# A relative attention's first unshifted scores made beside the phase before it, and a routing phase with its residual tiles made early

## What is computed

```python
# layer 2 (its attention is done before; this is the end of it and the MoE)
x = x + attention(h, ...)                       # ctx @ wo + bo
h = layernorm(x, ln2_scale, ln2_shift)
scores = h @ gate_w                             # 8 experts, the best 2 are taken
out = sum over the 2 experts of weight * (silu(h @ w1) * (h @ w2)) @ w3
# layer 3, relative attention with 16 heads of width 8
AC = einsum('bhid,bhjd->bhij', q + u_bias, k)
BD = _rel_shift(einsum('bhid,hjd->bhij', q + v_bias, rp))
attn = softmax((AC + BD) * scale);  out = attn @ v
```

## Time and profile before

| | |
|---|---|
| median of 3 runs | 1942.32 us (1934.86 to 1944.3) |
| profiled execution | 1947.51 us, of which 1945.9 us are the traced span |
| PE, DVE, ACT, POOL busy | 71%, 59%, 51%, 24% of the span |
| moved by DMA | 451.86 MB |
| `phase_route` to the start of `phase_blocks` | 535.5 to about 678 us |
| `phase_combine` | 828.1 to 959.6 us |
| `phase_relative` | 959.6 to 1833.3 us |

### The profile page before, as it was taken

One profiled execution on the slowest core, in us unless ns is written; L12 is line 12 of the kernel. 1 busy time (PEld: TensorE's weight loads), 2 busy tenths in 40 slices (PEclk: granted clock), 3 DMA queues, 4 the chain that ended last, 5 costly groups with the idle time before them and its releaser, 6 DMA issues. The chain is left out here.

```text
span 1945.9 us, 48913 instructions
## 1 busy us (share of the span) xinstructions
PE 1381.7 (71%) x18791; PEld 902.3 (46%) x18791; DVE 1147.5 (59%) x3054; ACT 1000.3 (51%) x1996; POOL 465.0 (24%) x762
## 2 busy tenths in 40 slices
PE   6636277777654269825458989888898989989646
PEld 3213144444334258713235655555555656556423
DVE  6953377777354223336326767766676766767637
ACT  4524056666612023313446767766676766767234
POOL 5443345555347610078000000000000000000033
PEclk9867589999955579966769999999998998999869
DMA  7429512222031176638899999999999999999531
GB/s 310 170 94 284 117 47 69 65 64 70 12 104 41 46 178 198 181 105 266 256 375 331 373 366 378 383 375 366 366 378 333 378 379 377 386 382 371 165 105 44
DMA packets 174816, 451.86 MB, mean 232 GB/s; under 512 B 41632, under 2 KB 133952, under 8 KB 157504
## 3 DMA queue, kind: packets, MB, share of 16 engines
q1 hardware_dynamic: 129488, 237.18, 37.1%
q10 hardware_dynamic: 32592, 180.39, 23.7%
q0 software_dynamic: 12512, 31.21, 6.0%
HBM read 222.59 MB, written 225.84 MB: 230 GB/s over the span
## 5 line engine op out<-in xcount | busy, mean ns | idle before, releaser
L2651 DVE CUSTOM_DVE_ANT_0 r_shifted<-r_ps_ac,r_shifted 128x512 f32<-128x512 f32 x512 | 351.9, 687 | 278.3 <-PE r_ps_ac L2530 236.4
L2617 ACT ACTIVATE r_probs<-r_ps_keys 128x512 f32<-128x512 f32 x512 | 309.6, 605 | 228.2 <-PE r_ps_keys L2537 203.3
L2596 ACT ACTIVATE r_wide<-r_ps_wide 128x512 f32<-128x512 f32 (+1 forms) x576 | 329.5, 590 | 63.6 <-PE r_ps_wide L2521 63.2
L2537 PE MATMUL r_ps_keys<-r_ident,r_shifted 128*128 128x128 f32 x2048 | 325.8, 283 | 16.8 <-issue 10.8
L2537 PEld LDWEIGHTS r_ps_keys<-r_ident,r_shifted 128*128 128x128 f32 x2048 | 267.4, 147 | 64.8 <-issue 19.6
L2521 PE MATMUL r_ps_wide<-r_r,r_qv 128*32 128x96 bf16 (+12 forms) x6144 | 235.7, 254 | 55.2 <-issue 40.3
L2659 DVE TENSOR_SCALAR r_shifted<-r_shifted,r_mx 128x512 f32<-128x512 f32 x512 | 249.2, 487 | 18.3
L985 ACT ACTIVATE c_probs<-c_ps_keys 128x512 f32<-128x512 f32 (+1 forms) x384 | 174.3, 530 | 130.9 <-PE c_ps_keys L911 130.7
L2530 PE MATMUL r_ps_ac<-r_k,r_qu 128*128 128x512 bf16 x512 | 207.8, 406 | 22.7 <-DMA r_k<-stack 20.6
L1190 POOL MEMSET n_zeros<- 128x4 f32 x1 | 0.1, 102 | 898.4 <-POOLq L2371 898.4
L2521 PEld LDWEIGHTS r_ps_wide<-r_r,r_qv 128*32 128x32 bf16 x6144 | 104.2, 98 | 153.2 <-issue 152.6
(11 more groups left out here) (253 smaller groups left out, 1920.3 us busy)
## 6 DMA issues: line engine op xcount, KB each, us to landing
skew<-r_wide ACTq DMA_DIRECT2D x64, 2224.0 KB, 13.5
r_shifted<-skew SPq DMA_DIRECT2D x64, 2160.0 KB, 14.4
by_expert<-a_blank ACTq DMA_DIRECT2D x4, 4352.0 KB
e_w<-in_L_ffn_w_dram SPq DMA_DIRECT2D x117, 128.0 KB, 2.4
c_qk<-qk_stacks POOLq DMA_DIRECT2D x64, 192.0 KB, 3.8
stack<-d_part SPq DMA_DIRECT2D x96, 128.0 KB
qk_stacks<-b_part SPq DMA_DIRECT2D x48, 128.0 KB, 3.3
qk_stacks<-b_part POOLq DMA_DIRECT2D x48, 128.0 KB, 3.7
```

Of the source, the lines that this page charges most:

```text
L2537: last = pe.transpose(ps_keys[u % 2][:, j * P:(j + 1) * P], shifted[:, s, W * u + j * P:W * u + (j + 1) * P], ident[:, :])
L2596: act.activation(wide[:, s, c, lo:hi], ps_wide[bk % BANKS][:, 0:hi - lo], ACT.Copy).then_inc(wide_sb, 1)
L2617: act.activation(probs[:, h % 2, :, b * P:(b + 1) * P], ps_keys[u % 2][:, :].rearrange("p (j i) -> p j i", j=NT), ACT.Exp, scale=SCALE).th ...
L2651: dve.tensor_tensor_reduce(out=shifted[:, s, W * u:W * u + L], in0=ps_ac[u % 2][:, :], in1=shifted[:, s, W * u:W * u + L], scale=1.0, scal ...
```

## The change

In `phase_route`: `xb` gets a tile for each batch and is made 2 ahead, then 3 batches at a time behind the roots of batches 0 and 1. The norm keeps two sets of moments and roots (`TurnNorm`). Minus the mean times the root is one instruction of DVE (`scale_means`), which stands behind `best` and ahead of `mark`, in place of two of POOL. The waits for the small tables move from the start of each engine's queue to their first use.

In `phase_combine`: the operands of step 0 (and the queries of step 1) are loaded behind batch 2's first two stores; the 18 banks of step 0 are made by PE and copied by ACT, five each in batches 3, 4 and 5 and three in batch 6; SP sends the two halves, in batches 5 and 7, ahead of those batches' `stack` stores. `phase_relative` starts with the fetches of step 0 and makes only step 1's banks ahead of its steps.

```diff
+def position_products(pe, ps, qv, r, s, g, c, bk):
+    lo, hi = BANK * bk, min(BANK * bk + BANK, CW)
+    for v in range(HT):
+        u = HT * c + v
+        h, b = u // NT, u % NT
+        for a in range(P // Q):
+            q0 = b * P + a * Q
+            start = W * v + P - Q - Q * a
+            split = start + q0 + Q
+            for one, frm, to in ((0, start, split), (1, split, start + W)):
+                frm, to = max(frm, lo), min(to, hi)
+                if frm < to:
+                    at = frm - start + L - Q - q0
+                    last = pe.matmul(ps[Q * a:Q * a + Q, frm - lo:to - lo], qv[:, s, h, q0 + one:q0 + one + Q],
+                                     r[:, g // 2, h, at:at + to - frm],
+                                     start=True, stop=True, skip_group_check=True)
+    return last
...
-                if n >= SLOTS:
-                    pool.wait_ge(xa_ready, n - SLOTS + 1)
-                pool.tensor_tensor(xb[:, n % SLOTS, :, :], x[:, n, :, :],
+                pool.tensor_tensor(xb[:, n, :, :], x[:, n, :, :],
...
-            AHEAD = 3
-            pool.memset(zeros[:, :], 0.0).then_inc(zeros_set, 1)
-            pool.wait_ge(zeros_set, 1)
+            AHEAD = 2
...
             for n in range(NB):
-                pool.wait_ge(norm.var_ready, n + 1)
-                pool.tensor_tensor(minus[:, n, :], zeros[:, :], norm.mv[:, :, 0], ALU.subtract)\
-                    .then_inc(minus_mean, 1)
-                if n >= 1:
-                    pool.wait_ge(z_ready, n)
-                norm.root(pool, n + 1)
-                pool.wait_ge(minus_mean, n + 1)
-                pool.wait_ge(norm.rstd_ready, n + 1)
-                pool.tensor_tensor(minus[:, n, :], minus[:, n, :], norm.rstd[:, :], ALU.mult)\
-                    .then_inc(minus_ready, 1)
-                if n + AHEAD < NB:
-                    add_bias(n + AHEAD)
+                if n >= 2:
+                    pool.wait_ge(z_ready, n - 1)
+                norm.root(pool, n)
+                for later in range(AHEAD + 3 * n, min(AHEAD + 3 * n + 3, NB)):
+                    add_bias(later)
                 if n >= 2:
                     scatter(n - 2)
...
-            pe.wait_ge(route_loaded, 16 * 5)
-            pe.wait_ge(patterns_set, 6)
-            pe.wait_ge(lower_set, 1)
...
                     invert(n + 2)
+                if n == 2:
+                    pe.wait_ge(patterns_set, 6)
+                    pe.wait_ge(lower_set, 2)
                 if n >= 2:
                     rank(n - 2)
+                if n == 1:
+                    pe.wait_ge(route_loaded, 16 * 5)
                 if n >= 1:
                     score(n - 1)
                 turn(n)
...
-                                  xb[:, n % SLOTS, :, :], ALU.add).then_inc(xa_ready, 1)
+                                  xb[:, n, :, :], ALU.add).then_inc(xa_ready, 1)
                 dve.wait_ge(xa_ready, n + 1)
-                if n >= 1:
-                    dve.wait_ge(minus_ready, n)
-                norm.moments(dve, xa[:, n % SLOTS, :, :], n + 1)
+                norm.moments(dve, xa[:, n % SLOTS, :, :], n)
...
+            def scale_means(n):
+                dve.wait_ge(norm.rstd_ready, n + 1)
+                dve.scalar_tensor_tensor(out=minus[:, n, :], in0=norm.mv[:, n % 2, :, 0], scalar=-1.0,
+                                         in1=norm.rstd[:, n % 2, :], op0=ALU.mult, op1=ALU.mult)\
+                    .then_inc(minus_ready, 1)
...
-            dve.wait_ge(route_loaded, 16 * 5)
-            dve.tensor_scalar(lower[:, :], mask[:, :], 0.0, None, ALU.is_lt).then_inc(lower_set, 1)
             divide(0)
             for n in range(NB):
                 if n + 1 < NB:
                     divide(n + 1)
                 merge(n)
+                if n == 0:
+                    dve.wait_ge(route_loaded, 16 * 5)
+                    dve.tensor_scalar(lower[:, :], mask[:, :], 0.0, None, ALU.is_lt).then_inc(lower_set, 1)
...
                     best(n - 1)
+                scale_means(n)
+                if n >= 1:
                     mark(n - 1)
...
+        BANKS = 3
+        ROWS = 64
+        WIDE_FROM = 3
+        WIDE_EACH = 5
...
+        def wide_banks(n):
+            first = WIDE_EACH * (n - WIDE_FROM)
+            return range(max(first, 0), max(min(first + WIDE_EACH, 2 * NBK), 0))
...
                 sp.dma_start(v9_out[n], v9[:, s, :, :]).then_inc(v_stored[s], 16)
+                if n == WIDE_FROM - 1:
+                    sp.wait_ge(stored[0], STORES)
+                    sp.wait_ge(act_stored[0], ACT_STORES)
+                    for g in range(2):
+                        sp.dma_start(qv_tile[ROWS * g:ROWS * g + SK, g, :, 0:L],
+                                     stacks_out[1].rearrange("b r (g h) t -> b g r h t", h=G)[0, g])\
+                            .then_inc(queries_loaded, 16)
+                    for dst, table in ((qu_tile, stacks_out[0]), (k_tile, stacks_out[2])):
+                        sp.dma_start(dst[0:SK, 0, :, :], table.rearrange("b r (g h) t -> b g r h t", h=G)[0, 0])\
+                            .then_inc(operands_loaded, 16)
+                for c in range(2):
+                    if n >= 1 and NBK * (c + 1) - 1 in wide_banks(n - 1):
+                        sp.wait_ge(wide_sb, NBK * (c + 1))
+                        dst = skew_out[c]
+                        sp.dma_start(bass.AP(tensor=dst.tensor, offset=dst.offset, ap=[[CW, P], [1, CW]]),
+                                     wide[:, c, :]).then_inc(sent, 16)
                 for c in range(NSP):
                     sp.wait_ge(part3_ready, NC * n + c + 1)
                     term_stores(sp, n, c, stored[s])
...
+            def wide_bank(i):
+                if i == 0:
+                    pe.wait_ge(queries_loaded, 32)
+                if i >= BANKS:
+                    pe.wait_ge(wide_sb, i - (BANKS - 1))
+                position_products(pe, ps_wide[i % BANKS], qv_tile, rel_r, 0, 0, i // NBK, i % NBK)\
+                    .then_inc(wide_ps, 1)
...
+            for ps in ps_wide:
+                for j in range(NT):
+                    pe.transpose(ps[:, j * P:(j + 1) * P], ident[:, :], ident[:, :])
             turn(0)
...
+                for i in wide_banks(n):
+                    wide_bank(i)
...
+            def copy_wide(i):
+                c, bk = i // NBK, i % NBK
+                act.wait_ge(wide_ps, i + 1)
+                lo, hi = BANK * bk, min(BANK * bk + BANK, CW)
+                act.activation(wide[:, c, lo:hi], ps_wide[i % BANKS][:, 0:hi - lo], ACT.Copy).then_inc(wide_sb, 1)
...
+                for i in wide_banks(n):
+                    copy_wide(i)
...
-            load_queries(0, 0)
-            load_queries(0, 1)
-            load(0, 0)
+            sp.sem_inc(stored, 64)
+            for s in range(2):
+                sp.sem_inc(qv_loaded[s], 16)
+            sp.sem_inc(loaded[0], 32)
+            for c in range(2):
+                sp.sem_inc(sent[0][c], 16)
+            fetch(0, 0, 0)
             load_values(0, 0)
-            sp.sem_inc(stored, 64)
-            for c in range(2):
-                fetch(0, 0, c)
-            sp.wait_ge(wide_ps, 2 * NBK)
+            fetch(0, 0, 1)
             load_queries(0, 2)
             load(0, 1)
...
-                last.then_inc(wide_ps, 1)
+                position_products(pe, ps, qv, r, s, g, c, bk).then_inc(wide_ps, 1)
...
-            for n in range(2):
-                pe.wait_ge(qv_loaded[n], 16)
-                for c in range(2):
-                    for bk in range(NBK):
-                        wide_bank(n, n, n, c, bk)
             pe.wait_ge(loaded[0], 32)
             content_tile(0, 0, 0)
             content_tile(0, 0, 1)
+            pe.sem_inc(wide_ps, 2 * NBK)
+            pe.wait_ge(qv_loaded[1], 16)
+            for c in range(2):
+                for bk in range(NBK):
+                    wide_bank(1, 1, 1, c, bk)
...
             steps(step, pe)```

In what follows, `x3` behind a row is a count. POOL's queue in `phase_route` (`m_norm_rstd` is a root, `m_xb` the residual plus bias of one batch, `by_expert` the 8 indirect transfers of one). Before, the rows of batch 2:

```order
L1465 TENSOR_TENSOR m_minus<-m_zeros,m_norm_mv 128x4
L123 TENSOR_TENSOR m_norm_var_eps<-m_norm_mv,m_norm_consts 128x4
L126 TENSOR_TENSOR m_norm_rstd<-m_norm_var_eps,m_norm_consts 128x4
L1472 TENSOR_TENSOR m_minus<-m_minus,m_norm_rstd 128x4
L1434 TENSOR_TENSOR m_xb<-m_x,m_bo 128x512
L1442 DMA by_expert<-m_z,m_pos 34816x128 x8
```

More of the change, by code:

```diff
@@ L41 @@
 CW = HT * W + P - Q
+BANK = 512
+NBK = -(-CW // BANK)
 REGION = NB * L
@@ L1893, in _, with phase_combine @@
             take_sums(BLOCKS - 1)
-def phase_combine(nc, sems, tiles, y_in, w_in, biases, tables, ident_in, x_out, stacks_out, v9_out):
+def phase_combine(nc, sems, tiles, y_in, w_in, biases, tables, ident_in, x_out, stacks_out, v9_out,
+                  relative):
     base, pos, pr = tiles
+    qu_tile, k_tile, qv_tile, rel_r, skew_out = relative
```

(12 more changed lines are left out.)

41 lines of the change are left out of this document (15 added, 26 removed).

## The result

The changed kernel takes 1929.35 us (median of 12 runs, 1916.28 to 1932.33) against 1945.69 (12 runs, 1934.86 to 1958.22): ratio 0.9898, interval 0.9873 to 0.9923. The ratio is not the quotient of the two medians, which is 0.9916: by the medians the change is 16 us faster, by the ratio 20 us, 0.8 to 1.0%. The forecast was 1922 in a range of 1908 to 1935. Three later sets of runs, each on another chip of the three, had the changed kernel in two of them: 0.9900 (0.9866 to 0.9935) in the second set and 1.0011 (0.9981 to 1.0041) in the third, where the gain is gone. Both have to be explained. The chip of the first result is not on record.

A forecast was written before the change was run, and what follows sets the result against it. DMA engines bound phase_relative, PE close behind; POOL bounds phase_route. Routing 8.9 plus combine and relative 11 gives 20 us off the profiled 1947.5, so 1927.5, or 1922 us against the median 1942.3; range 1908 to 1935.

The forecast's parts named there:

- Routing, 8.9 us: phase_route: earlier start 3.4 us, roots' batches 7.5 us, less 2.0 us of cost; between 2 and 12 us gained.
- the gaps between scatters: phase_route, POOL: without the additions and two minus instructions, the gaps between scatters shrink by 5.8 us in all.
- The chain for one batch: phase_route: best experts to next moments takes about POOL's new period, 11.6 us; the gain could fall to 4 us.
- The meeting: phase_route, batches 0 and 1: DVE's scale_means is released exactly when POOL begins xb, 1.0 us lost each.
- (c): phase_route: POOL's additions hold up scale_means in batches 0 and 1; first scatter 2 us later, 0 to 7 us.
- The banks, 0 (0 to 4): phase_combine: step 0's banks are hidden in PE's and ACT's slack and cost nothing, bounds 0 to 4 us.
- The cover is thin: phase_combine: slack barely hides ACT's added copies; at 0.7 us or more a bank, four batches slip about 1 us each.
- The sends, 7.5 us: End of phase_combine: 11 us for two sends less 3.6 us of idle DMA time; 7.5 us longer, 3 to 29.
- The start of relative, 11 us net: Start of phase_relative: idle DMA time and moved operand loads, 14.9 us less 4; 11 us gained, 4.1 to 23.8.
- PE's first bank of step 2: Start of phase_relative, a sign: this bank comes about 15 us behind the phase's start.
- PE's lead is kept: phase_relative, rival: held by PE's order as much as by DMA, PE's 23.8 us lead stays; 1908 us, chance 0.15.
- Slower through SP's blocked queue: phase_combine, rival: stores wait behind sends, combine ends 29 us later and more; 1952 us at 41 us delay, chance 0.05.

The follow-up runs named there:

- e3: The changed kernel with all eight residual tiles added on POOL ahead of the first root; 1931.82 us, ratio 0.9900 to before.
- e1: Before with the edits of phase_route alone; 1940.25 us, ratio 0.9952 to before.
- e10: Before with step 0's eighteen banks and operand loads also in combine, nothing sent, relative unedited, run in the third set; 1973.68 us, ratio 1.0143 to before.
- e6: Before with step 0's eighteen banks and operand loads also in combine, nothing sent, relative unedited, run in the first set; 1980.62 us, ratio 1.0150 to before.
- e7: Before with step 0's banks, loads and both sends from SP also in combine, relative unedited; 1978.84 us, ratio 1.0165 to before.
- e5: The changed kernel with step 2's queries and step 1's content operands issued ahead of the fetches in relative; 1921.57 us, ratio 0.9877 to before.
- e4: The changed kernel with both sends issued by ACT behind a half's last copy, in place of SP; 1922.40 us, ratio 0.9873 to before.
- e8: The changed kernel itself, run again in the third set; 1954.57 us, ratio 1.0011 to before.
- e9: Before with the edits of phase_combine and phase_relative alone, run in the third set; 1957.36 us, ratio 1.0024 to before.

## Why the prediction was right, and where it was not

**Routing, 8.9 us: right, 9.8.** Up to the first scatter 4.2 us (40.5 to 36.3 us into the phase) against 3.4 + 1.75 - 2.0 = 3.15; the rest in the gaps between scatters (5.6 against 5.8), which shrank to 1.53 us as the earlier trace rows said. The chain for one batch did not bite. The meeting came in both batches, in batch 1 on a cast of DVE ahead of `scale_means` (1.21 us, 0.18 in e3) and on the marks behind it (`x_hot` twice in 1.31 us, 0.29 in e3). The price (c) was still near 1 us net: the first projection came 3.6 us earlier in the phase, and 3.6 + 1.75 - 4.2 = 1.1. As I read it, e3's 2.2 us is the price against no meeting at all, and before had paid one already, the 1.19 us of `m_both`. The Trainium skill (SBUF — State Buffer, section "SBUF: two separate sides") has it, for a DVE instruction with two SBUF inputs, as a lock for a whole instruction: 1.23 us under POOL's addition and 0.16 without it agree. The cast has one input, so this part of the rule does not speak of it, and no run shows what held it. e1 gave 8.0 to 9.4 us by itself on a chip with late signals, whose trace has only 6.7 of it in routing.

**The banks, 0 (0 to 4): right in the result and the second set, wrong in the other two.** The step "The cover is thin: if a bank took 0.7 us or more, each of four batches would slip by about 1 us" named the right place and the wrong cause. A bank takes 0.5 us everywhere. What can be late is PE's signal, mostly by 2 to 7 us and at most by 11.5 (e10), and a batch with banks waits for several in a row where the old one had slack; the term is 21 us there (20.9 and 21.0 in e6 and e10). No row of before could show this, since its trace has no late signal.

**The sends, 7.5 us: right in the traces.** In the span of combine e7 less e6 gives 7.6 us, and 7.5 against e10; the whole times are too uncertain to show it. The whole growth of combine, 10.1 us, was under-sized by 2.6, which I put down to the border and the loads; no run separates these.

**The start of relative, 11 us net: right in size, or 3 us too high.** By the bytes of the first trace it is 21.3 - 10.1 = 11.2 us; by the three traces at before's rate it is 18 - 10.1 = 8 us. The forecast's own parts were 18.5 us off relative (11 + 7.5) and 7.5 on combine, so by these traces relative came out as summed and the 2.6 us too few of combine are the miss. The part was never timed by itself where no signal was late, so it rests on the phases and the bytes. PE's first bank of step 2 was forecast 15 us behind the phase's start and came at 25.7, since I had overlooked that in the new order its queries stand behind both fetches again. It cost nothing in the sum, because I had taken the sum from the DMA engines' time and not from PE's order, and e5 fits that: with the wait of 11.93 us gone 4 to 7 us come by the bytes.

**The rivals.** *PE's lead is kept* (1908) seemed true by the first trace, 24.6 us for combine and relative; 13 of it is the rate, and the medians, 16 and 20 us in all, leave 7 to 11 beside routing. *Slower through SP's blocked queue* falls with e4. What happened in the first and the third set, a new combine that eats the gain, was in none of them; its balance in e8: 4.3 us gained in routing, 30.0 lost in combine, 25.3 gained in relative, together 0.4 lost, with the rate at 374 GB/s. That the forecast was met in the first result is therefore in part luck: the record holds one set of runs in which the same kernel gains nothing.

## What to carry to other kernels

When a phase is bound by DMA throughout, price a moved transfer by its bytes: what is done elsewhere, and what the idle start now moves, over the rate, gave 21.3 us, and traces at one rate 18, where the spans of two executions gave 35. Compare the rates of two traces before their spans. Work that is free in one engine's slack still adds signals between engines; in two sets of three PE's signals beside GpSimd's indirect transfers came some 5 us late. So I would put a hand-over in short steps where no such transfers are issued (not tried here), and time a gain of 1% on more than one chip.

## What the runs showed of the hardware beyond this

On the chips of the first and the third set signals of PE to ACT and DVE came late, with waits of up to 11.5 us, and all those marked "remote" end while GpSimd issues indirect transfers or within 3 us of the last; the time of before hardly moved (1948.25 and 1949.42 us there, 1945.69 and 1946.96 in the other two comparisons). It is in the untraced runs too: the changed kernel's medians are 1929, 1927 and 1955. What differs between the chips is open. That GpSimd's transfers are the cause is argued from the times alone, since no run takes them away, and before itself was not traced on a chip with late signals. Open too is whether banks beside batches 6 and 7, behind the last gather, keep the gain there: the rows for batches 5 and 6 say so, and it was not tried. Banks alone are 28 to 29 us slower by the ratios, with 21 in combine. In the traces the difference is the rate again: e6's relative, unedited, took 892.4 us at 363 GB/s and e10's 877.4 at 370, against 873.7 at 372 and e7's 866.2 at 375, and time by rate gives 272 to 273 MB for the steady part of all four.

A send of 2224 KB adds 5 us to the issue of the 12 stores behind it, and 4 to 7 us on a queue that it does not stand in (12.64 and 14.83 us for 12 in e4, 8.31 in the batch between). The DMA rate in the steady part varied between executions of one program from 374 (e8) to 379 GB/s, over all kernels with the new relative from 371 (e9) to 379, and with the old from 363 (e6) to 375 (e7), at a share of 0.99 or more. Over 265 MB the first two are 9 and 15 us; the third is 24 us over 273 MB. What sets the rate is open.
